# Softmax of the routing in two parts, first convolution group by group, and the decay table scaled later, in a fused language-model tower on one core

## What is computed

```
# stage 1: tokenizer
h   = gelu(conv7(onehot, w1) + b1); h = gelu(conv5(h, w2) + b2)
ctx = sigmoid(conv3(h, w3) + b3)
amps = emb[id] * ctx ; lp = locality_shapes[id] ; center = place + 0.05*lp0
for s in 4 scales: z = (position - center)/width_s
                   basis += exp(-z*z/2) * cos(phase + 2*pi*z) * gain * weight_s**2
h = einsum("bsp,bsd->bpd", basis, amps)
# stage 2: state space layer on layernorm(h), complex poles, 64 states, then h += Re(C * state)
# stage 3: experts on layernorm(h)
H = gelu(xf @ W1 + b1) ; probs = softmax(H @ Wg + bg)  # 8 experts
e = argmax(probs) ; h += probs[e] * (H @ Wd[e] + bd[e])
```

## Time and profile before

| what | value |
|---|---|
| median of three runs (lowest, highest) | 112.77 us (111.68, 113.23) |
| the profiled execution's own time | 111.52 us |
| its span, first to last instruction | 109.6 us |
| TensorE busy, share of span | 100.5 us, 92% |
| VectorE | 90.0 us, 82% |
| ScalarE | 70.8 us, 65% |
| GpSimd | 51.0 us, 47% |
| granted clock of TensorE | 1.000 throughout (its upper level, 2.4 GHz) |

### The profile page before, as it was taken

How to read it: one execution, slowest core, us unless ns; L and a number is a source line. 1 busy time by engine, 2 the same in 40 slices (tenths; PEclk the granted TensorE clock), 3 DMA queues, 4 the chain that set the end, 5 groups by cost and what they waited for, 6 DMA issues and landing times.

```text
span 109.6 us, 2018 instructions
## 1 busy us (share of the span) xinstructions
PE 100.5 (92%) x723; PEld 64.3 (59%) x723; DVE 90.0 (82%) x230; ACT 70.8 (65%) x126; POOL 51.0 (47%) x101
## 2 busy tenths in 40 slices
PE   5979999999999978869899999999999799999970
PEld 2356785364434576347567477876696476776640
DVE  0359999999999949999999599678999956199892
ACT  4604599999999999999869438454758513551000
POOL 7798998899980007205509426256005000000670
PEclk9999999999999999999999999999999999999999
DMA  3999700000000100000000000000000000000044
GB/s 91 269 233 408 283 0 0 3 0 0 6 0 4 5 0 0 0 0 6 0 0 0 0 6 0 0 0 0 0 0 9 0 0 0 0 0 0 0 96 96
DMA packets 4313, 4.15 MB, mean 38 GB/s; under 512 B 3280, under 2 KB 3536, under 8 KB 4176
## 3 DMA queue, kind: packets, MB, share of 16 engines
q1 hardware_dynamic: 4160, 3.92, 12.5%
q10 hardware_dynamic: 144, 0.12, 0.4%
HBM read 3.50 MB, written 0.52 MB: 37 GB/s over the span
## 4 chain that ended last, share of the span: by engine, by line
PE 42%; ACT 38%; DVE 8%; DMA 4%; issue 4%; POOL 2%; ACTq 0%; DVEq 0%
PE pair L1080 14%; ACT wave L476 8%; PE bank L1042 7%; ACT bell L466 7%; ACT bell L470 5%; ACT L425 5%; DMA ids<-x 4%; DVE pair L819 3%; PE hid_pair L1053 3%; PE pair L951 3%; ACT angle L514 3%; PE pair L921 2%; ACT h L460 2%; PE hid_pair L1063 2%; ACT dist L455 2%
## 5 line engine op out<-in xcount | busy, mean ns | idle before, releaser
L379 POOL TENSOR_SCALAR var_eps<-mean_var 128x4 f32<-128x4 f32 x8 | 3.7, 458 | 33.0 <-DVE mean_var L747 33.0
L819 DVE COPY_PREDICATED pair<-later,pair 128x256 f32<-128x256 int32 (+3 forms) x30 | 12.3, 409 | 5.3 <-PE pair L1080 4.6
L921 PE MATMUL pair<-warm 128*128 128x512 bf16 x53 | 13.3, 380 | 0.0
L732 DVE SCALAR_TENSOR_TENSOR bell<-bell,scale_w,wave 128x512 f32<-128x512 f32 x16 | 10.8, 743 | 0.0
L1080 PE MATMUL pair<-wd_high,H_high 128*128 128x512 f32 x32 | 10.8, 418 | 0.0
L921 PE MATMUL hid_pair<-warm 128*128 128x512 bf16 x30 | 9.0, 455 | 1.3 <-POOL warm L298 1.3
L1080 PE MATMUL pair<-wd_low,H_high 128*128 128x512 f32 x32 | 10.0, 394 | 0.0
L395 POOL TENSOR_TENSOR angle<-picked,prob 128x256 f32<-128x256 f32 x3 | 1.8, 613 | 17.2 <-DVE prob L843 17.2
L521 ACT ACTIVATE bell<-hid_pair,sm 128x512 f32<-128x512 f32 x8 | 5.0, 680 | 7.2 <-PE hid_pair L1053 7.2
L675 DVE TENSOR_TENSOR wave<-dist,inv_width 128x2048 f32<-128x2048 f32 x4 | 9.3, 2356 | 0.0
L965 PE MATMUL pair<-h,w_sb 128*64 128x512 f32 x40 | 9.1, 597 | 0.0
(11 more groups left out here) (166 smaller groups left out, 226.1 us busy)
## 6 DMA issues: line engine op xcount, KB each, us to landing
ids<-x SPq DMA_DIRECT2D x2, 512.0 KB, 5.7
posb<-positions SPq DMA_DIRECT2D x1, 768.0 KB, 8.1
wd_sb<-wd SPq DMA_DIRECT2D x1, 512.0 KB, 9.1
out<-angle SPq DMA_DIRECT2D x3, 128.0 KB, 2.0
st_sb<-state SPq DMA_DIRECT2D x1, 328.0 KB, 8.3
w_sb<-w SPq DMA_DIRECT2D x1, 256.0 KB, 6.6
posb<-positions SPq DMA_DIRECT2D x1, 256.0 KB, 6.6
w_sb<-w SPq DMA_DIRECT2D x1, 160.0 KB, 8.0
```

Source lines behind the costliest of these rows:

```text
L732: ins = dve.scalar_tensor_tensor(out=bell[:, g, part], in0=bell[:, g, part], scalar=scale_w[:, s:s + 1], in1=wave[:, g, part], op0=ALU.mul ...
L819: return dve.copy_predicated(held[:, :, 0:n, 0, 0:D], repeat(later[:, g, 2 * h + rows.start:2 * h + rows.stop, first:first + n], 3, D), he ...
L921: pe.matmul(bank[free], warm[:, 0:P], warm[:, :], start=True, stop=True)
```

## The change

The scaling of `decay` moves on ScalarE from before the `C_part` tables to behind `taps_out(1)` and `gaussian(2)`. TensorE's first convolution is done one group at a time: part 0 and part 1 of group 0, then of group 1, and so on. The softmax is split: `softmax_in(0)` for groups 0 to 2 stands behind `route(2)`, `probability(0)` behind `split_hidden(3)`, and part 1 (group 3) takes the places where the whole stood. ScalarE loads the table of the exponential by a one-element instruction behind `round_hidden(3)`, takes the first exponential ahead of `gate_out(3)` and the second behind it. `finish(0)` on GpSimd, whose text is unchanged, waits for `s_prob` to be 1, which is now the first part; VectorE's last group waits for 2.

```diff
+        early_or_last = (slice(0, G - 1), slice(G - 1, G))
...
+            def exponentials(last):
+                act.wait_ge(s_below, last + 1)
+                act.activation(expl[:, early_or_last[last]], below[:, early_or_last[last]],
+                               ACT.Exp).then_inc(s_expl, 1)
...
             square(1)
             act.wait_ge(s_poles, 1)
-            act.wait_ge(s_ones_decay, 1)
-            act.activation(decay[:, :, :], decay[:, :, :], ACT.Copy, scale=spar[:, 2:3]).then_inc(s_decay, 1)
             act.wait_ge(ld["state"], 16)
...
             taps_out(1)
             gaussian(2)
+            act.wait_ge(s_ones_decay, 1)
+            act.activation(decay[:, :, :], decay[:, :, :], ACT.Copy, scale=spar[:, 2:3]).then_inc(s_decay, 1)
             upright_out(1)
             context_out(1)
...
             round_hidden(3)
+            load_exp()
+            exponentials(0)
             gate_out(3)
-            act.wait_ge(s_below, 1)
-            act.activation(expl[:, :, :, :], below[:, :, :, :], ACT.Exp).then_inc(s_expl, 1)
+            exponentials(1)
...
-            def softmax_in():
-                link(dve.tensor_tensor(top[:, :, :], ladder[:, :, :, 12], ladder[:, :, :, 13], ALU.max))
-                dve.tensor_tensor(below[:, :, :, :], logits, repeat(top[:, :, :], 3, NE),
+            def softmax_in(last):
+                part = early_or_last[last]
+                link(dve.tensor_tensor(top[:, part], ladder[:, part, :, 12], ladder[:, part, :, 13], ALU.max))
+                dve.tensor_tensor(below[:, part], logits[:, part], repeat(top[:, part], 3, NE),
                                   ALU.subtract).then_inc(s_below, 1)
...
-            def probability():
-                dve.wait_ge(s_expl, 1)
-                link(dve.tensor_reduce(denom[:, :, :].rearrange("p g b -> p (g b)"),
-                                       expl[:, :, :, :].rearrange("p g b e -> p (g b) e"),
+            def probability(last):
+                part = early_or_last[last]
+                dve.wait_ge(s_expl, last + 1)
+                link(dve.tensor_reduce(denom[:, part].rearrange("p g b -> p (g b)"),
+                                       expl[:, part].rearrange("p g b e -> p (g b) e"),
                                        mybir.AxisListType.X, ALU.add))
-                dve.reciprocal(prob[:, :, :], denom[:, :, :]).then_inc(s_prob, 1)
+                dve.reciprocal(prob[:, part], denom[:, part]).then_inc(s_prob, 1)
...
             route(2)
+            softmax_in(0)
             pick(1, 1)
             pick(2, 0)
             split_hidden(3)
+            probability(0)
             route(3)
-            softmax_in()
+            softmax_in(1)
             pick(2, 1)
-            probability()
-            dve.wait_ge(s_prob, 1)
+            probability(1)
+            dve.wait_ge(s_prob, 2)
...
-            conv1((0, 1))
-            conv1((2, 3))
+            for g in range(G):
+                conv1((g,))
             conv2(0)
```

## The result

The changed kernel took 113.37 us (median of six runs, 112.73 to 113.97); six runs of the kernel before, three of which are those of the table above, had a median of 113.0 us (111.53 to 114.96). Some runs of the kernel before were slow ones (up to 114.96) and are left out of the ratio of the two kernels, which is 1.0156 with a 95% interval of 1.0112 to 1.0200. So by these runs the change costs 1.1 to 2.0%, about 1.3 to 2.3 us. The changed kernel's six runs lie in two lots, three at 112.73 to 112.83 and three at 113.90 to 113.97. The kernel before took 111.65 us in the median of the eighteen runs that were made later beside run f1, so the first lot is 1.1 to 1.2 us above it. The forecast of 114.2 on a median of 112.77 was 1.3%.

The account below looks back on a forecast made before the run. No single engine bounds the kernel: PE and ACT share the chain, DVE sets the end. +0.35 (decay) + 0 + 1.1 (GpSimd's finishing) + 0 = +1.45 us on 112.77 gives 114.2 us, range 112.5 to 115.2.

Parts of the forecast that it names:

- What bounds the kernel: Whole kernel: no single engine; PE and ACT share the chain, and DVE sets the end after 0.24 us idle.
- Conv 1: First convolution: group 0 complete after 8 matmuls, ACT gains a lead of at most 1.0 us; PE's conv 2 unchanged.
- Decay: Scaling moved behind gaussian(2): 0.16 us of ACT's lead left at conv2_out(0), gates(1), outputs(0) and the end +0.35 us.
- First softmax part and probability(0): softmax_in(0) behind route(2) costs nothing; probability(0) ahead of route(3) alone costs 0 to 0.1 us, taken as 0.
- GpSimd's finishing: Finishing now beside the ladder of route(3) and softmax_in(1): blocked ladder instructions make the last picks +1.1 us, bounds 0 and 1.7.
- Stores: Last store is alone at the end: taken as 0, with a gain of up to 0.5 us as the bound.
- The third rival: Store drain at the end: the last store, alone, lands earlier, making the kernel faster, 112.6 us; chance 0.08.
- Without collision: GpSimd's finishing doesn't slow the ladder; only the decay counts, 113.1 us; chance 0.24.
- The heavy case: In the ladder, two short gaps go to GpSimd: +1.7 us plus the decay's 0.35, 115.0 us; chance 0.14.
- The sum +1.45 us: Whole change: +0.35 (decay) + 0 + 1.1 (GpSimd's finishing) + 0 (stores), forecast 114.2 us.

Follow-up runs that it names:

- f1: Changed kernel with GpSimd's finish held until softmax_in(1) is done and the decay in its old place: median 111.58 us against 111.65, ratio 0.9998 to the kernel before.
- e4: Changed kernel with GpSimd's first finish also waiting for softmax_in(1): ratio 1.0085 to the kernel before, span 109.8 us.
- e1: Kernel before, with only the decay scaling moved behind gaussian(2): ratio 1.0074, span 109.9 us.
- e3: Kernel before, with only the softmax split: ratio 1.0069, span 110.3 us.
- scratch streams: Kernel before, with GpSimd chains on scratch rows after split_hidden(3): four products took 114.44 us, end +1.09 us; with seven copies, end +0.46 us.

## Why the prediction held, point by point

- **What bounds the kernel.** Right. The delay made at 46 us arrived at the end in full, that made at 100 us less the time for which VectorE had been waiting for TensorE ahead of the last picks.
- **Conv 1.** Right: group 0 came 0.94 us earlier by the marks (12.88 - 10.59 against 13.59 - 10.36), and TensorE's second convolution stopped what the wait at square(0) had left of the lead; 0.13 to 0.15 us survive against 0.16 forecast.
- **Decay.** Right: +0.35 us at gates(1) and at outputs(0), and +0.32 alone. Forecast +0.35. Less the start of this execution, gates(1) began at 45.84, as worked out.
- **First softmax part and probability(0).** Right, by e4: with the collision removed the end is at +0.04 of before.
- **GpSimd's finishing.** The mechanism is shown (e1, e3 and e4 account for the whole, the scratch streams make it without the split). The term was mis-sized: +1.1 forecast, +0.82 measured. The order of who gets in first was off. L804 (now L812), which the sum had blocked, started in the same 0.01 us as the stream and passed; L805 (now L813) met it instead, so the blocks fell on L813, L820 and L821. They cost 0.30 + 0.42 + 0.38 us against instructions of 0.17 to 0.19. pick(2, 1) came 0.2 us earlier than worked out, and the last picks followed the end of probability(1) after 0.03 us and not 0.1. The scratch stream, which starts 0.17 us ahead of its L809, shows the first two blocks of the forecast (L804 and L807), but its third falls on L812 and not on L811. That it costs 1.09, near the forecast's 1.1, is in part chance: its blocks sum to 1.26 us and other waits stand behind them.
- **Stores.** Right to take 0: 0.1 us in the changed kernel and none in the mended version. The third rival (0.5 us) falls. The section of the Trainium skill that the prediction names against it (DMA: Bandwidth & Descriptors, Anatomy of one DMA — SWDGE (gpsimd) path) is about DMAs that GpSimd issues, and these stores are issued by SyncE. What speaks for a cost that hardly depends on the size here are their own rows: 2.0 us for 128 KB, 1.6 to 1.8 for 64 KB.
- **The rivals.** Without collision (113.1): refuted by the ladder's rows and by e4, though the runs' median of 113.37 alone would have looked like it; its companion, the median of before, had moved by then from 112.77 to 113.0. The heavy case: L812 and L815 did start in their gaps, so 1.10 us were lost in the ladder and not 1.7. TensorE's second pair waited for pick(2, 1), by 0.2 us where the forecast had 0.5, and VectorE didn't wait for it, as forecast.

The sum +1.45 us stands between what the profiles show (1.1 to 1.2) and the middle of what the runs' ratio gives (1.8). On the scale of the profiled executions the forecast was 112.97 us and 112.73 was measured. The forecast of 114.2 is further off, 0.8 us above the median, because it was built on 112.77 us, the median of three scattered runs; the later 111.65 would have given 113.1.

## What to carry to other kernels

An earlier start of work on a side engine isn't free because that engine was idle: ask which instructions of the bounding engine it will now run beside, and whether they share a way into memory. A chain of short instructions can suffer much, as each can be held to the end of a stream several times its length. When an instruction is moved to where an engine "has time", the place is right only if nobody waits for what stands behind it; two instructions further on the same work holds up nobody there. And two edits that each remove time ahead of the same wait don't add up.

## What the runs showed of the hardware

The Trainium skill (SBUF — State Buffer, Who interferes with whom) says that VectorE's second pair of ports is GpSimd's only one. The Trainium skill adds, on the same page under SBUF: two separate sides, that VectorE instructions with two inputs in SBUF contend only with GpSimd instructions that read SBUF. Both fit these runs: the fills (2.9 us beside the ladder) blocked nothing, products and copies of 256 elements did.

The Trainium skill also says, in the first of these sections, that the pair is held for a whole instruction. That doesn't fit the powers: the first power on four elements ran from 98.72 to 99.73 us, and four ladder instructions beside it took 0.17 to 0.19 us. A ladder instruction of 4 to 32 elements that was hit ended within 0.05 us of the product or copy beside it, one of 128 elements some 0.15 us behind it. That the block goes with the data streamed, and not with the kind of instruction, is a reading that fits; a GpSimd product on four elements, which would test it, wasn't run beside the ladder.

Of five ladder instructions three were hit, both in the changed kernel and beside the scratch products, and four beside the copies. In every case it was the engine that started first that got through, be it by a hundredth of a microsecond. L815 started 0.03 us ahead of GpSimd's sum and wasn't held; among the scratch products L810 started 0.02 us ahead of the second (101.07 against 101.09) and wasn't held. Beside the copies L816 started 0.01 us behind the third (99.66 against 99.65) and L817 0.01 us behind the fourth (100.13 against 100.12), and both were held. Where both started in the same 0.01 us (L812 of the changed kernel, at 99.62; L816 beside the products, at 101.92; L810 beside the copies, at 99.15) VectorE got through. So a gap of 0.05 to 0.08 us between two streams doesn't let a VectorE instruction in by itself; it has to be the first to start.
